# A selective scan and a mixture of experts in one kernel: another order for the side work between the scans

## What is computed

```
# block 1, a selective state-space scan (512 inner channels, 16 states)
xn = x * rsqrt(mean(x*x) + 1e-6) * norm_w
x_inner, gate = split(xn @ in_proj_w)
x_inner = x_inner * silu(gate)
xc = causal depthwise convolution of x_inner, 4 taps
dt = softplus(xc @ dt_w + dt_b);  A = -exp(A_log);  Bm = xc @ B_w;  Cm = xc @ C_w
h = exp(dt*A) * h + dt*Bm*xc            # per channel and state, along 1024 tokens
y = sum over the states of h*Cm, + D_skip*xc;  out = y @ out_proj_w
# block 2, a mixture of 8 experts, the 2 best for each token
top_p, top_i = top-2 of softmax over x @ gate_w
expert_out = sum of top_p * (silu(x @ Wg) * (x @ Wu)) @ Wd
shared = (silu(x @ Sg) * (x @ Su)) @ Sd
```

## Time and profile before

| | us |
|---|---|
| median of 3 runs | 1810.65 (1805.61 to 1811.26) |
| the profiled execution | 1814.42 |
| its span, first to last instruction | 1812.6 |
| mean granted clock of PE, as a share of full speed | 0.945 |
| scans, first to last | 80.3 to 1118.8 |
| chunk 2, first scan to the next chunk's first | 134.8 |
| expert tiles and last norm, from about | 1180 |

### The profile page before, as it was taken

The page is one execution under the profiler, slowest core; times in us unless marked ns, Lnnn a source line. Parts: engine busy times, 40 slices in busy tenths (PEclk is TensorE's granted clock), DMA queues, the critical chain, the costliest instruction groups (busy, mean ns, idle before and its releaser), DMA issues.

```text
span 1812.6 us, 23920 instructions
## 1 busy us (share of the span) xinstructions
PE 1569.5 (87%) x7068; PEld 1057.0 (58%) x7068; DVE 1152.0 (64%) x1928; ACT 854.1 (47%) x1480; POOL 1046.7 (58%) x1233
## 2 busy tenths in 40 slices
PE   5888798898898898898898768699999999999990
PEld 2354555555555655655555645467777777777770
DVE  2299998898898898898898997222222222222225
ACT  3566657657658657658657554222112222121214
POOL 0579779779778779778778885312222222222224
PEclk9899899999999999999999968799999999999995
DMA  3111112211211111111111652514212222222216
GB/s 96 48 35 48 47 47 73 73 48 49 73 45 55 65 46 58 65 42 58 60 48 47 219 157 73 171 42 113 43 33 34 33 33 34 34 34 34 34 28 191
DMA packets 84393, 116.21 MB, mean 64 GB/s; under 512 B 11120, under 2 KB 58576, under 8 KB 84272
## 3 DMA queue, kind: packets, MB, share of 16 engines
q1 hardware_dynamic: 63344, 82.94, 14.6%
q0 software_dynamic: 16704, 27.57, 7.8%
q10 hardware_dynamic: 4224, 4.19, 0.7%
HBM read 81.05 MB, written 33.10 MB: 63 GB/s over the span
## 4 chain that ended last, share of the span: by engine, by line
PE 37%; DVE 5%; issue 4%; POOL 3%; ACT 2%; DMA 1%; DVEq 0%; POOLq 0%; ACTq 0%; SPq 0%
PE A L1255 10%; PE bA L1214 9%; PE bH L1214 9%; DVE arena L862 2%; PE bY L1238 2%; POOL arena L1019 1%; PE bH L592 1%; DVE arena_t L879 1%; DMA sum_scratch<-arena_t 1%; PE A L1246 1%; PE A L522 1%; PE A L1238 1%; PE A L577 1%; PE A L564 1%; PE A L555 1%
## 5 line engine op out<-in xcount | busy, mean ns | idle before, releaser
L1019 POOL TENSOR_TENSOR arena<-arena 128x512 f32<-128x512 f32 x512 | 645.5, 1273 | 175.5 <-DVE arena L862 173.0
L736 ACT ACTIVATE bA<-arena,a_neg 128x512 f32<-128x512 f32 x512 | 353.6, 692 | 284.0 <-DVE arena L862 278.7
L592 PEld LDWEIGHTS bH<-ident,arena 128*128 128x128 f32 x2048 | 260.8, 149 | 316.9 <-issue 147.6
L592 PE MATMUL bH<-ident,arena 128*128 128x128 f32 x2048 | 336.0, 292 | 89.0 <-DVE arena L862 75.5
L862 DVE TENSOR_TENSOR_SCAN arena<-bA,arena 128x512 f32<-128x512 f32 x256 | 305.8, 1209 | 45.0 <-ACT bA L736 32.1
L862 DVE TENSOR_TENSOR_SCAN arena<-bA,hl,arena 128x512 f32<-128x512 f32 x256 | 322.0, 1270 | 13.9 <-ACT bA L736 13.9
L1350 POOL DMA_INDIRECT sum_scratch<-arena_t x71 | 113.5, 1598 | 187.1 <-issue 156.5
L1386 ACT ACTIVATE arena_t<-bA 128x352 f32<-128x352 f32 x142 | 58.1, 461 | 322.3 <-PE bA L1214 322.3
L1255 PE MATMUL A<-arena,hT 128*128 x852 | 195.8, 379 | 0.8 <-ACT hT L1392 0.8
L1344 POOL DMA_DIRECT2D arena_t<-expert_in_scratch x71 | 40.7, 573 | 257.7 <-PE A L1246 208.2
L1214 PE MATMUL bA<-arena,arena_t 128*128 x568 | 179.8, 459 | 1.3 <-ACT arena_t L1397 1.3
(11 more groups left out here) (194 smaller groups left out, 2118.4 us busy)
## 6 DMA issues: line engine op xcount, KB each, us to landing
arena<-b_scratch SPq DMA_DIRECT2D x128, 256.0 KB, 3.2
arena_t<-expert_in_scratch POOLq DMA_DIRECT2D x71, 132.0 KB, 2.4
arena<-in_L_ffn_Wg_dram SPq DMA_DIRECT2D x8, 704.0 KB, 6.0
arena<-in_L_ffn_Wu_dram SPq DMA_DIRECT2D x8, 704.0 KB, 7.1
arena<-in_L_ffn_Wd_dram SPq DMA_DIRECT2D x8, 640.0 KB, 8.2
arena<-in_L_attn_x_dram SPq DMA_DIRECT2D x8, 512.0 KB, 4.9
arena_x<-in_L_attn_x_dram SPq DMA_DIRECT2D x8, 512.0 KB, 5.0
x_scratch<-arena_x SPq DMA_DIRECT2D x8, 512.0 KB, 3.2
```

The source lines that it names most:

```text
L592: i = e.transpose(bH[g % NH][:, q * P:(q + 1) * P], hh[:, (n - 1) % 2, q, d * P:(d + 1) * P], ident[:])
L736: e.activation(bA[g % NA][:], dt[c % 2][:, d, :], ACT.Exp, scale=a_neg[:, d, n:n + 1]).then_inc(s_a, 1)
L1019: e.tensor_tensor(bb[:, k % NB, :], u[c % 2][:, d, :], br[:, n % NR, :], ALU.mult).then_inc(s_bb, 1)
```

## The change

Only tables and two conditions change.

```diff
-LEAD = {"xnT0": 61, "xnT1": 62}
-PROJ = {"gate0": 0, "gate1": 2, "gate2": 9, "gate3": 11, "inner0": 13, "inner1": 15, "inner2": 17, "inner3": 19,
-        "cv0": 21, "cv1": 24, "cv2": 27, "cv3": 30, "bT": 33, "dt0": 36, "bc": 38, "dt1": 40, "dt2": 44, "dt3": 49}
-POST = {"y0": 4, "y1": 6, "y2": 7, "y3": 8, "out0": 10, "out1": 16, "xfT0": 47, "xfT1": 48, "logit": 51, "rank": 58, "sg0": 52, "sg1": 54, "sg2": 56,
-        "su0": 57, "su1": 59, "su2": 63, "sd0": SLOTS + 3, "sd1": SLOTS + 5}
-
-ACT_AT = {"gate": (2, 4, 11, 13), "silu": 13, "conv": (24, 27, 30, 33), "bT": 36, "bc": 39, "dt": (40, 44, 48, 53),
-          "root_x": 52, "norm_x": (59, 59, 59, 59), "xnT": (62, 63), "out": (14, 20), "root_out": 25, "norm_out": (32, 32, 32, 32),
-          "root_xf": 39, "xf": (45, 45, 45, 45), "xfT": (48, 49), "e2": 58, "sg": (54, 56, 58), "sg_silu": 58,
-          "sd": (SLOTS + 5, SLOTS + 7), "sum": 3}
-DVE_AT = {"stats_x": 48, "inner": (16, 18, 20, 22), "y": (5, 7, 8, 9), "stats_out": (16, 22), "stats_xf": 35, "logit": 52, "max": 53, "index": 54,
-          "place": 59, "base": 60, "position": 62, "sgs": (60, 61, SLOTS + 1)}
-POOL_AT = {"var_x": 50, "norm_x": 54, "halo": 5, "skip": 37, "dt": (43, 47, 51, 56), "var_out": 24, "norm_out": 28, "add": (33, 33, 33, 33), "var_xf": 37, "norm_xf": 41,
-           "diff": 55, "token": 50, "chosen": 57, "picked": 61, "gates": SLOTS, "scatter": SLOTS + 2}
+LEAD = {"xnT0": 61, "xnT1": 61}
+PROJ = {"gate0": 2, "gate1": 1, "gate2": 9, "gate3": 9, "inner0": 12, "inner1": 18, "inner2": 20, "inner3": 18, "cv0": 21, "cv1": 23, "cv2": 26,
+        "cv3": 30, "bT": 33, "dt0": 36, "bc": 37, "dt1": 42, "dt2": 45, "dt3": 50}
+POST = {"y0": 8, "y1": 6, "y2": 5, "y3": 6, "out0": 10, "out1": 13, "xfT0": 47, "xfT1": 46, "logit": 51, "rank": 60, "sg0": 56, "sg1": 55, "sg2": 53,
+        "su0": 58, "su1": 62, "su2": 62, "sd0": SLOTS + 3, "sd1": SLOTS + 7}
+
+ACT_AT = {"gate": (4, 3, 11, 11), "silu": 14, "conv": (26, 25, 28, 33), "bT": 36, "bc": 42, "dt": (40, 45, 49, 53), "root_x": 51,
+          "norm_x": (55, 55, 55, 55), "xnT": (60, 61), "out": (16, 19), "root_out": 27, "norm_out": (30, 31, 31, 31), "root_xf": 39,
+          "xf": (41, 44, 44, 45), "xfT": (50, 46), "e2": 60, "sg": (58, 57, 55), "sg_silu": 58, "sd": (SLOTS + 5, SLOTS + 8), "sum": 3}
+DVE_AT = {"stats_x": 48, "inner": (15, 19, 24, 21), "y": (9, 7, 5, 7), "stats_out": (19, 22), "stats_xf": 34, "logit": 52, "max": 54, "index": 54,
+          "place": 59, "base": 59, "position": 62, "sgs": (60, 63, SLOTS)}
+POOL_AT = {"var_x": 50, "norm_x": 53, "halo": 7, "skip": 36, "dt": (43, 49, 51, 58), "var_out": 23, "norm_out": 28, "add": (31, 31, 31, 31),
+           "var_xf": 38, "norm_xf": 40, "diff": 55, "token": 47, "chosen": 56, "picked": 61, "gates": SLOTS, "scatter": SLOTS + 1}
@@ def sp_lead
-        if k == 44:
+        if k == 24:
@@ def pool_proj, at POOL_AT["skip"]
-            all_emptied(e, CONVS, c)
+            emptied(e, f"cv{ND - 1}", c)
```

## The result

| | before | after |
|---|---|---|
| median, us | 1810.76 (1805.61 to 1811.26, 4 runs) | 1750.46 (1748.44 to 1751.45, 4 runs) |
| ratio, 95% | | 0.9672 [0.9652, 0.9692] |
| the profiled execution, its span | 1814.42, 1812.6 | 1749.59, 1747.5 |
| first scan's start, last scan's end | 80.3, 1118.8 | 79.1, 1054.6 |
| chunk 2, first scan to the next chunk's | 134.8 | 125.6 |

The change gains 60 us.

What follows compares the result with a forecast made beforehand. VectorE was taken as nearly the bound, PE right behind, so its idle time could be won. The terms, 21 - 4 + 8 - 5 + 4 + 3.5 - 4 = 23.5 us gained, gave 1787 us against the median, range 1768 to 1806.

Steps and rivals of the forecast that it cites:

- the norm of x: ScalarE's slot 59 to 55: scan 58 about 1 us late, 0.35 us spared; cost 4 us, bounds 0 and 9.
- slots 9 to 24: Counted for slots 9 to 16: PE crowded, sums late, silu's stall halved; net cost 5 us.
- the norm of the output: Moved to 30/31 from 32: waits around slots 33/34 lose about half; 4 us gained, bounds 0 and 8.
- The cause of slot 59: POOL's late mm_ holds rank on PE and e2 on ScalarE; earlier mm_, later readers gain 21 us, bounds 14 and 28.
- slot 1: su1 and su2 at slot 62 fill idle PE, so the half clock's cost to VectorE goes: 4 us gained.
- The wait only moves: Rival, 20%: mm_ in time, but freed time lost to decays and PE in slots 9 to 16; 8 us gained, 1803.
- It doesn't do what it says: Rival, 4%: POOL stays late, e2 and the ranks still wait; 1810 us.
- The rows for the router: Their norm spread over slots 41, 44, 45: a 0.59 us decay wait goes; 3.5 us gained, bounds 0 and 4.
- dt3's gap: dt3 one slot later leaves PE idle, then crowded; sum 53 some 0.7 us late, 4 us lost, bounds 0 and 8.
- Slots 5 to 8: New order of y with sd1 behind relieves PE in slots 5 and 6: 4 us gained; slot 8's wait stays.
- PE's crowding decides: Rival, 8%: PE falls to half clock in slots 9 to 14 and at dt3; 12 us slower, 1823.
- All relief adds up: Rival, 13%: half clock of slots 59 to 1 goes wholly, every chunk like chunk 7; 42 us gained, 1769.

Runs made afterwards that it cites:

- z_rank_e2: Kernel before with rank at PE's slot 60, place at VectorE's 60 and e2 at ScalarE's 60: 0.9864, 24.5 us gained.
- x_end: Kernel before with only the change's table entries for slots 50 to 63: 1782.16 us, 0.9845.
- y_norm59: Changed kernel with the norm of x back at ScalarE's slot 59 and its transposes and their copies back too: 1758.24 us, 0.9716.
- z_gates: Kernel before with gate3 at PE's slot 9 beside gate2, both copies in ScalarE's slot 11: 1806.24 us, 0.9977.
- x_start: Kernel before with only the change's table entries for slots 0 to 24, with the convolutions: 1794.22 us, 0.9900.
- y_silu13: Changed kernel with the gate's silu back at ScalarE's slot 13 instead of 14: 1759.03 us, 0.9718.
- z_start4: Kernel before with gate3 early, silu at ScalarE's slot 14, out copies from 16, inner0 on VectorE at 15, stats_out at 19: 1808.65 us, 0.9998.
- z_normout: Kernel before with only the output's layernorm in its new slots (27, 30/31, 23, 31): 1798.44 us, 0.9937.
- y_fill: Kernel before in its own order, with useless repeated matmuls on PE at gate2 and xnT1: 1809.51 us, 0.9989.

## Why the prediction was wrong, step by step

The gain is 60 us and not 23.5. Three terms make nearly all of the difference: the norm of x (12 us off), slots 9 to 24 (18) and the norm of the output (some 7).

**The cause of slot 59 and its removal: right.** e2 and L544 wait for nothing, and VectorE idles 1.7 us at slots 59 and 60 in chunk 1, within the 1 to 2.5 that I had named. My terms here were 21 us and 4 for slot 1. The slots measured 30, but 9.3 of that are the norm of x and its transposes (below), so the relief itself is about 21; z_rank_e2 puts it at 24.5. "The wait only moves" and "It doesn't do what it says" fell: x_end alone is worth 28 us. What I hadn't said is that the term is one of two arms: 2 and 9 us apart, 24.5 together.

**The norm of x: the sign was wrong, by 12 us.** I counted 4 us of cost, a scan 58 that waits 1 us for its decay. It waits for nothing, and y_norm59 measures 8 us of gain. The step that failed is "slot k of ScalarE starts when scan k ends". It starts when scan k-1 ends, and makes the decay of scan k+1; the front's "2 slots ahead" is wrong in the same way, it is one. In the trace of after, ScalarE in chunk 2:

```profile
344.35 0.69 ACT L735 ACTIVATE bA<-arena,a_neg 128x512 f32<-128x512 f32 x1 [0.42 <-DVE arena L861]
345.06 1.28 ACT L640 ACT_TABLE_LOAD   x1
346.35 1.91 ACT L640 ACTIVATE arena<-arena 128x2048 f32<-128x2048 f32 x1
348.28 1.28 ACT L641 ACT_TABLE_LOAD   x1
349.58 1.30 ACT L735 ACTIVATE bA<-arena,a_neg 128x512 f32<-128x512 f32 x2
```

The silu is in slot 14. The decay in front of it is that of scan 15, released by the end of scan 13; the first one behind it is that of scan 16. So each block of ScalarE stood one slot off from where I laid it against VectorE. At 55 the norm runs beside max and index, which VectorE does behind scan 54. Scan 56 waits for its decay in chunks 2 and 4 alone, 1.4 us in each, and with the norm back at 59 it waits the same 1.4 us for the last columns. So the norm costs nothing there. Of the gain, 4.1 us are the decay of scan 61, for which I had counted 0.35 a chunk; the 5.6 of slot 63 are PE's, a term that I didn't have.

**Slots 9 to 24: the sign was wrong, by 18 us.** Two entries of the term failed. First, PE's crowding: I counted sums 11, 13 and 14 late by 2.6 us a chunk, 15.6 in six; in after VectorE waits 5.1 us for tiles of PE in slots 9 to 24, and 8.4 before. z_gates gains 4 us, and in x_start, the whole block, the gain is 18. Second, the silu's stall: I halved it, since it would fall into the same time as the late sums; the decay's wait behind the silu went from 13.1 to 1.7 us. What VectorE and ScalarE have beside it I didn't count. With the true offset it can be read from the tables. Beside a silu in slot 13 VectorE has, from the end of scan 12, two scans and two sums. Beside one in slot 14 it has, from the end of scan 13, two scans, three sums and inner0 (0.68 us), and the copies of a gate and of out0 (0.6 us each) are no longer in the same stretch. In after, the scan behind the silu waits 0.57 us:

```profile
349.05 0.68 DVE L783 TENSOR_TENSOR arena<-arena,A 128x512 f32<-128x512 f32 x1
350.30 2.34 DVE L861 TENSOR_TENSOR_SCAN arena<-bA,arena 128x512 f32<-128x512 f32 x2 [0.57 <-ACT bA L735]
```

Before, in the same chunk:

```profile
360.79 1.22 DVE L862 TENSOR_TENSOR_SCAN arena<-bA,arena 128x512 f32<-128x512 f32 x1 [2.02 <-ACT bA L736]
```

The silu's slot alone is worth 8.6 us in the new order (y_silu13). z_start4 shows that this reading isn't the whole: out0's copy and inner0 did win 6.5 us, and lost more through out0's bank; in the change out1 stands in front of inner1.

**The norm of the output: right mechanism, sized 4, measured 11 to 12.** I halved the 1.16 us wait of the earlier trace rows and didn't follow it to its cause. The cause is a PE wait of 1.88 us for the last convolution's copy, and VectorE waits in three slots, not one: 2.1 us in slot 33 for a decay behind the norms, 6.7 and 1.2 us in slots 34 and 35 for PE. All three are gone in z_normout.

**Small terms.** The rows for the router 3.5 against 4.4; dt3's gap 4 of cost against 1.1. Slots 5 to 8 came out as 3.4 against 4 by luck: the waits for PE in slots 5 and 7 went wholly (6.9 us), and the wait for the last columns, which I had left as it was, doubled in slot 7 (4.1 to 8.5). Over all six chunks it went from 10.1 to 14.0 us, a sign against me that I had named; x_end shows it too, 8.7 us in slot 7, so most of it comes with the end block.

**"PE's crowding decides" fell, and so did the clock's part in it.** The granted clock rose to 1.00 in the six chunks. The Trainium skill (TensorE: Matmul & The Clock Gate, Part 1: The HAM clock gate) states that the throttled state is the default and activity releases it. This trace agrees as far as it goes: with PE's waits gone, half clock fell from 68 to 7 us. The double payment for new gaps that I drew from that rule didn't occur, since the waits before the ranks (18.3 us) and for out0's bank (10.7 us) are gone. A new one came, which I had named as a sign against me: xnT1 waits for su0's bank, 9.9 us in six chunks. In chunk 1 the clock behind this gap of 2.1 us was 1.00, so not every gap was followed by half clock. It doesn't reach VectorE, whose slots 61 and 62 have no wait for PE there:

```profile
PE A L439 <- DVE arena_x L847: 9.9, 5, 2.1
```

y_fill puts the clock's own share in slots 1 and 13 at 9 us; that of slot 59 stays open.

**The sum.** With the measured sizes in place of mine (-30, -3.4, -13.1, -11.6, -4.4, +1.1, 0, -4.8) and the +1 of the other slots it is 65 us in the profiles, less the 3.7 and 0.9 that they lie apart from their medians: about 60. The mechanism with the most chance was right for slot 59. "All relief adds up", at 42 us, came nearest, and it too lacked the gains at slots 9 to 24 and 33. My range ended at 1768 because no term but that of slot 59 had a bound large enough. I had said that VectorE's idle would fall from 86 to about 62 us; all its waits together fell to 36. My bound of 85.9 us for a perfect order stands: 57 of the 92.9 us of VectorE's waits went.

## What to carry to other kernels

Before a side piece is costed in its slot, find in one timeline which scan's end releases that slot and which instruction of the bound engine runs beside it; one slot of error turned the norm's sign here and hid the silu's gain. When one late producer holds two engines, neither relief alone shows its value (9 and 2 us against 24.5 together), so test the pair. And where banks are used in turn, a piece that is emptied later also needs the piece three places on to come later, or the wait only changes engines, as in z_start4.

## What was unexpected of the hardware

Half clock on TensorE was cheap: y_fill took 31 of 68 us of it away in six chunks and won 9, and VectorE's waits there were 10.5 us in all. I read this as the transposes being made ahead of their sums. And in an in-order stream a fuller engine was the faster one: with two gates together PE had more to do in slots 9 to 12, and VectorE's waits for it in slots 9 to 24 fell from 8.4 to 5.1 us in six chunks, 4.8 of them in slot 14. A table load costs ScalarE 1.28 us and no more: in the rows of after above, 345.06, 346.35, 348.28 and 349.58 follow on each other without a gap.
